# A Mamba-2 phase on one NeuronCore: the recurrence's products split, batched and moved a slot ahead

## What is computed

```python
x = x + 0.5 * ffn(layernorm(x)); x = x + mamba2(layernorm(x)); x = x + 0.5 * ffn(layernorm(x))

def mamba2(h):       # 64 heads of 64, state 128, 2 batches x 1024 tokens
    z, xBC, dt = split(h @ W_in.T)
    x, B, C = split(silu(conv4(xBC) + conv_b))
    # per chunk of tokens l, s <= l in the chunk, A_cum the running sum of dt * A:
    Y_diag = (C_l . B_s) * exp(A_cum_l - A_cum_s) @ (x * dt)
    states = B^T @ (exp(A_cum_end - A_cum) * x * dt)
    new    = prev * exp(A_cum_end) + states          # prev is zero before the first chunk
    Y_off  = exp(A_cum_l) * (C_l . prev)
    g = (Y_diag + Y_off + D * x) * silu(z)
    return rmsnorm(g) * norm_w @ W_out.T
```

## Time and profile before

| | |
|---|---|
| median of 3 runs | 2496.81 us (2495.47 to 2498.77) |
| the profiled execution, first to last instruction | 2493.7 us |
| Mamba phase within it | from 352.6 (first of its records) to about 2131 us |
| TensorE busy, whole span | 91% |
| VectorE, ScalarE, GpSimd busy | 69%, 58%, 59% |
| mean granted TensorE clock, share of full | 0.968 |

### The profile page before, as it was taken

The page is one execution under the profiler, slowest core; times in us unless marked ns, Lnnn a source line. Parts: engine busy times, 40 slices in busy tenths (PEclk is TensorE's granted clock), DMA queues, the critical chain, the costliest instruction groups (busy, mean ns, idle before and its releaser), DMA issues. The chain is left out here.

```text
span 2493.7 us, 44179 instructions
## 1 busy us (share of the span) xinstructions
PE 2278.8 (91%) x11910; PEld 1779.2 (71%) x11910; DVE 1725.5 (69%) x3562; ACT 1437.7 (58%) x2899; POOL 1474.0 (59%) x1306
## 2 busy tenths in 40 slices
PE   5799977999999999999888999999999998579997
PEld 3677765777777777777566777777777776358776
DVE  6432276788887878788877788878878787653226
ACT  5133326676676766776556776667767775413332
POOL 2876342666666666666426666666666665178533
PEclk8999989999999999999899999999999999689999
DMA  8665342332333334334213333343333332165545
GB/s 334 236 190 161 125 143 60 89 89 89 94 105 86 86 92 105 88 88 97 66 41 95 89 88 97 97 96 88 88 93 101 84 88 51 52 232 187 161 134 192
DMA packets 204905, 285.33 MB, mean 114 GB/s; under 512 B 16288, under 2 KB 148458, under 8 KB 204816
## 3 DMA queue, kind: packets, MB, share of 16 engines
q1 hardware_dynamic: 185936, 219.18, 31.6%
q0 software_dynamic: 18880, 65.02, 8.4%
HBM read 225.43 MB, written 58.72 MB: 114 GB/s over the span
## 5 line engine op out<-in xcount | busy, mean ns | idle before, releaser
L1306 POOL TENSOR_TENSOR mamba_mix<-mamba_mix,mamba_scores 128x512 f32<-128x512 f32 x256 | 330.8, 1292 | 272.8 <-ACT mamba_mix L1490 272.8
L1989 PE MATMUL mamba_p_proj<-mamba_xt_lo,mamba_in_hi 128*128 128x512 f32 x1056 | 462.2, 438 | 7.0 <-DVE mamba_xs L1683 5.2
L1990 PE MATMUL mamba_p_proj<-mamba_xt_hi,mamba_in_hi 128*128 128x512 f32 x1056 | 415.9, 394 | 0.0
L1991 PE MATMUL mamba_p_proj<-mamba_xt_hi,mamba_in_lo 128*128 128x512 f32 x1056 | 415.5, 394 | 0.0
L1486 ACT ACTIVATE mamba_mix<-mamba_cum_l,mamba_cum_g 128x128 f32<-128x128 f32 x1024 | 324.4, 389 | 0.6 <-issue 0.6
L1678 DVE SCALAR_TENSOR_TENSOR mamba_xs<-mamba_p_proj,mamba_taps,mamba_xs 128x511 f32<-128x511 f32 (+2 forms) x384 | 285.4, 743 | 36.3 <-ACT mamba_xs L1420 27.2
L1709 DVE TENSOR_TENSOR mamba_total<-mamba_p_out,mamba_total 128x512 f32<-128x512 f32 x256 | 177.0, 692 | 147.9 <-PE mamba_p_out L2025 143.3
L1300 POOL TENSOR_TENSOR mamba_xend<-mamba_xdt,mamba_to_end_g 128x512 f32<-128x512 f32 x128 | 160.8, 1257 | 198.8 <-DVE mamba_xdt L1736 198.8
L660 DVE TENSOR_TENSOR ffn_h<-ffn_p_gu,ffn_sil 128x256 f32<-128x256 f32 x110 | 46.9, 426 | 295.6 <-ACT ffn_sil L545 295.3
L1989 PEld LDWEIGHTS mamba_p_proj<-mamba_xt_lo,mamba_in_hi 128*128 128x128 f32 x1056 | 200.8, 190 | 62.2 <-issue 9.4
L1991 PEld LDWEIGHTS mamba_p_proj<-mamba_xt_hi,mamba_in_lo 128*128 128x128 f32 x1056 | 199.7, 189 | 45.0
(11 more groups left out here) (335 smaller groups left out, 5466.6 us busy)
## 6 DMA issues: line engine op xcount, KB each, us to landing
mamba_cum_l<-mamba_cum_rows SPq DMA_DIRECT2D x128, 512.0 KB, 5.9
mamba_rise<-mamba_exp_rows SPq DMA_DIRECT2D x256, 128.0 KB, 5.4
ffn_xs<-slots_in SPq DMA_DIRECT2D x78, 256.0 KB, 2.7
slots_out<-ffn_y SPq DMA_DIRECT2D x78, 256.0 KB, 2.4
mamba_raw_x<-in_t SPq DMA_DIRECT2D x34, 512.0 KB, 7.3
mamba_raw_z<-in_t SPq DMA_DIRECT2D x32, 512.0 KB, 8.0
mamba_raw_out<-out_t SPq DMA_DIRECT2D x32, 512.0 KB, 3.7
slots_out<-ffn_xs SPq DMA_DIRECT2D x1, 9984.0 KB, 41.9
```

The lines of the kernel that those rows point to most:

```text
L1306: pool.tensor_tensor(mix[:, c % 2, :, :], mix[:, c % 2, :, :], scores[:, b * CPB + c, :].unsqueeze(1).broadcast_to([P, GH, P]), ALU.mult). ...
L1989: pe.matmul(bank, in_hi[:, piece, kk, :], xt_lo[:, kk, c], start=(kk == 0), stop=False)
L1990: pe.matmul(bank, in_hi[:, piece, kk, :], xt_hi[:, kk, c], start=False, stop=False)
L1991: last = pe.matmul(bank, in_lo[:, piece, kk, :], xt_hi[:, kk, c], start=False, stop=(kk == KT - 1))
```

## The change

- `recur(c)` is split. `off(c)` issues the two products with the state, `start(c)` the 256-column one, and `diag(j)` the half-width products of chunks 2j and 2j + 1 together, eight in a row. `diag(0)` stands behind `project_x` tile 0, `diag(1)` behind `project_x` tile 1 (in slot 0 behind `project_z` tile 0).
- `off(0)` of b = 0 (state zero) and `start(3)` of b = 1 (state never read) go, with their `carry`, `decay_state`, `next_state` and the clearing of `state`; after a batch's first chunk of a group the state is a copy.
- `mix` gets four buffers, and ScalarE and GpSimd make the next unit's decays in this slot: `exponents(next, 0)`, `(1)`, `(2)`, `(3)` and `next_scores(0)` to `(3)`. Slot 0 makes six of them.
- The half-width products of a whole unit lie in `p_diag` (two banks), the state's in `p_off`, the upper half of `p_st`'s bank. `carry` covers the unit.
- VectorE: `carry_of(c)` and `next_state(c)` come first in the slot and again behind the three steps of `conv(0)`; the additions of D x are two of 512 columns (`add_skip`), behind `diag(1)`; `add_carry` is two of 512 columns (384 for b = 0). `stage` is split: `cum_g` is copied early in slot b = 1.
- ScalarE: `round_out` first, `high` of the two tiles on either side of `tap_x` tile 0. GpSimd: `this_out` early. SyncE: `load_cum` runs a slot ahead, so `load_in` now stands behind the load for the chunks 2 and 3 of the next b = 1.

The diff, cut (`decay_scores`, `exponents` and `decay_state` differ in indices and wait counts alone; `exponents` now waits for `s_diag` of the unit before):

```diff
@@ -1063,18 +1063,18 @@
-        mix = sb("mix", [P, 2, GH, P])
-        carry = sb("carry", [P, 2, CT, P])
+        mix = sb("mix", [P, CPB, GH, P])
+        carry = sb("carry", [P, CT, BLK])
...
+        p_diag = ps("p_diag", [P, CT, BLK])
+        p_off = p_st[:, GC:2 * GC].rearrange("p (h l) -> p h l", h=CT)
...
@@ -1342,38 +1351,45 @@
-                decay_state(0)
-                decay_scores(U, b, 1)
+                def next_scores(c):
...
+                if first:
+                    decay_scores(U, b, 2)
+                decay_x(k, gi, b, 1, first)
+                decay_state(k, gi, b, 1)
+                if first:
+                    decay_scores(U, b, 3)
                 clear(0)
                 next_z(0)
-                decay_x(k, gi, b, 1, first)
-                decay_state(1)
                 next_z(1)
-                decay_scores(U, b, 2)
+                this_out(0)
+                this_out(1)
                 clear(1)
-                this_out(0)
-                if last:
-                    this_out(1)
-                decay_state(2)
-                next_x(0)
-                decay_scores(U, b, 3)
+                decay_state(k, gi, b, 2)
+                next_scores(0)
+                if not first:
+                    add_squares(U - 1, 1 - b, 0, second)
+                next_scores(1)
+                if b == 0:
+                    decay_state(k, gi, b, 3)
                 clear(2)
                 if not first:
-                    add_squares(U - 1, 1 - b, 0, second)
+                    add_squares(U - 1, 1 - b, 1)
                 if last and k + 1 < batches:
                     first_dt(k + 1)
                     for ct in range(CT):
                         first_x(k + 1, 0, ct)
-                decay_state(3)
+                next_x(0)
+                next_scores(2)
                 clear(3)
-                if not first:
-                    add_squares(U - 1, 1 - b, 1)
-                if not last:
-                    this_out(1)
                 next_x(1)
+                if b == 0:
+                    decay_state(k, gi, 1, 0)
                 if not last:
                     decay_x(k, gn, bn, 0)
-                    decay_scores(U + 1, bn, 0)
+                next_scores(3)
...
@@ -1527,23 +1544,30 @@
+                if first:
+                    for c in (2, 3):
+                        exponents(k, gi, b, c, young=True)
+                if b == 1:
+                    for ct in range(CT):
+                        round_out(k, gi, U, ct, k == 0 and second)
                 if not first:
-                    for ct in range(CT):
-                        high(U - 1, gp, 1 - b, ct, second)
+                    high(U - 1, gp, 1 - b, 0, second)
                 if not last:
                     tap_x(k, gn, bn, 0, first)
-                exponents(k, gi, b, 2)
+                if not first:
+                    high(U - 1, gp, 1 - b, 1, second)
+                if not last:
+                    exponents(k, gn, bn, 0)
+                if b == 0 and not last_group:
+                    round_x(k, gi, V, 0)
+                if not last:
+                    exponents(k, gn, bn, 1)
+                    tap_x(k, gn, bn, 1, first)
                 if not first:
                     for ct in range(CT):
                         square(U - 1, 1 - b, ct)
-                if b == 1:
-                    for ct in range(CT):
-                        round_out(k, gi, U, ct, k == 0 and second)
-                elif not last_group:
-                    round_x(k, gi, V, 0)
                 if not last:
-                    tap_x(k, gn, bn, 1, first)
-                exponents(k, gi, b, 3)
+                    exponents(k, gn, bn, 2)
...
                     silu_z(U + 1, 1 - b, 1, first)
-                    exponents(k, gn, bn, 0)
-                    exponents(k, gn, bn, 1)
+                    exponents(k, gn, bn, 3)
...
@@ -1745,32 +1770,40 @@
-                def combine(c):
...
+                def carry_of(c):
+                    if (b, c) == (0, 0):
+                        return
+                    dve.wait_ge(s_st, U * CPB + c + 1)
+                    if c % 2 == 0 or (b, c) == (0, 1):
                         dve.wait_ge(s_rise[c // 2], U * 32 + 32)
...
+                    dve.tensor_tensor(carry[:, :, c * P:(c + 1) * P], p_off,
                                       rise[:, c // 2, :, c % 2 * P:(c % 2 + 1) * P], ALU.mult).then_inc(s_car, 1)
...
+                def next_state(c):
+                    if (b, c) == (NB - 1, CPB - 1):
+                        return
+                    ends = p_st[:, 0:GC].rearrange("p (h d) -> p h d", h=GH)
+                    dve.wait_ge(s_st, U * CPB + c + 1)
+                    if (b, c) == (0, 0):
+                        dve.tensor_copy(state[:, :, :], ends).then_inc(s_state, 1)
+                    else:
+                        dve.wait_ge(s_decayed, faded(k, gi, b, c))
+                        dve.tensor_tensor(state[:, :, :], ends, decayed[:, :, :], ALU.add).then_inc(s_state, 1)
+                def add_skip(ct):
+                    dve.wait_ge(s_diag, U * 2 + 2)
+                    dve.scalar_tensor_tensor(xs[:, b, ct, :], xs[:, b, ct, :], skip[:, bass.ds(gi * CT + ct, 1)],
+                                             p_diag[:, ct, :], ALU.mult, ALU.add).then_inc(s_y, 1)
+                def add_carry(ct):
+                    lo = (1 - b) * P
+                    dve.wait_ge(s_car, carried(k, gi, b, CPB - 1))
+                    dve.wait_ge(s_y, U * CT + ct + 1)
+                    dve.tensor_tensor(xs[:, b, ct, lo:BLK], xs[:, b, ct, lo:BLK], carry[:, ct, lo:BLK],
...
@@ -1798,40 +1831,43 @@
+                carry_of(0)
+                next_state(0)
                 if not first:
                     gate(k, gp, bp)
-                combine(0)
+                elif k > 0:
+                    finish(k - 1, range(6, T))
+                if b == 1 and not last:
+                    stage_cum(k, gn)
+                next_rows(0, 1)
+                next_stats(0)
+                conv(0, (1, 2, 3))
+                carry_of(1)
+                next_state(1)
                 if not first:
                     gate_low(U - 1, gp, 1 - b)
-                elif k > 0:
-                    finish(k - 1, range(6, T))
-                next_rows(0, 1)
-                conv(0, (1,))
-                next_stats(0)
-                add_carry(0)
-                combine(1)
-                conv(0, (2,))
-                conv(0, (3,))
-                add_carry(1)
                 next_rows(2, 3)
-                conv(1, (1,))
-                next_stats(1)
                 if last:
                     add_out(0)
-                combine(2)
+                add_skip(0)
+                carry_of(2)
+                next_state(2)
                 if last and not more:
                     add_out(1)
-                conv(1, (2, 3))
-                add_carry(2)
+                conv(1, (1, 2, 3))
+                next_stats(1)
                 next_rows(4, 5)
                 if more:
                     add_out(1)
-                combine(3)
+                add_skip(1)
+                carry_of(3)
+                next_state(3)
+                for ct in range(CT):
+                    add_carry(ct)
...
@@ -2059,28 +2096,44 @@
-                def recur(c):
...
+                def off(c):
+                    if (b, c) == (0, 0):
+                        return
                     s = (b * CPB + c) * P
...
+                    pe.wait_ge(s_state, carried(k, gi, b, c))
+                    if k > 0 or not (first and c == 1):
+                        pe.wait_ge(s_car, carried(k, gi, b, c) - 1)
                     for ct in range(CT):
...
+                        mm = pe.matmul(p_off[:, ct, :], state[:, 2 * ct:2 * ct + 2, :].rearrange("p h d -> p (h d)"),
+                                       bc[:, 1, s:s + P], start=True, stop=True)
+                    if (b, c) == (NB - 1, CPB - 1):
+                        mm.then_inc(s_st, 1)
+                def start(c):
+                    if (b, c) == (NB - 1, CPB - 1):
+                        return
+                    if (b, c) == (0, 0) and not first:
+                        pe.wait_ge(s_car, carried(k, gi, 0, 0))
                     if c % 2 == 0:
                         pe.wait_ge(s_xend, U * 2 + c // 2 + 1)
                     pe.matmul(p_st[:, 0:GC], b_rows[:, b * CPB + c, :],
                               xend[:, c, :, :].rearrange("p h d -> p (h d)"), start=True,
                               stop=True).then_inc(s_st, 1)
+                def diag(j):
+                    pe.wait_ge(s_mix, U * CPB + 2 * j + 2)
+                    pe.wait_ge(s_xdt, U * 2 + j + 1)
+                    if j == 0 and not first:
+                        pe.wait_ge(s_y, U * CT)
+                    for c in (2 * j, 2 * j + 1):
+                        for h in range(GH):
```

(23 more changed lines are left out.)

140 lines of the change are left out of this document (56 added, 84 removed).

## The result

| | before | after |
|---|---|---|
| median of four runs, us | 2497.1 (2495.5 to 2498.8) | 2405.1 (2402.2 to 2408.3) |
| profiled execution, us | 2493.7 | 2404.5 |
| slots 1 to 29, first and second batch, us | 738.5, 738.7 | 695.3, 697.8 |

What follows compares the result with a forecast made beforehand. TensorE, 91% busy, was taken as the bound: slots fall from 25.46 to 23.48 us, 115 us over 58 slots, plus 5, 1 and 4 at the ends, 125 in all, giving 2372 us; range 2343 to 2425.

Steps and rivals of the forecast that it cites:

- The forecast's floor: TensorE's loop slot without waits: 24.30 us before, less 0.43 and 0.74, gives 23.13.
- the removed terms: TensorE, one whole-width pair of eight and one L2081 of eight gone in two slots: 0.43 us a slot.
- the excursions: TensorE's changes to half width and back, four become two a slot: 2 x 0.37 = 0.74 us saved.
- what would show it: List of signs for right or wrong, such as slots 23.2 to 23.8 us apart and sixteen half-width records over 0.98 us.
- rival C: Eight half-width products over two banks no longer run in pairs: 1.74 us more a slot, 2473 us; chance 0.04.
- The waits for `mix` and the state: TensorE's waits for decayed scores and state: `mix` wait goes; no wait for the state at off(2) or off(3).
- Rival D: Slower: carry_of(1) and next_state(1), behind conv(0), come 5 us late; slot 27.2 us, total 2598; chance 0.05.
- VectorE's chain to `project_z` of tile 1: conv(1) ends 0.3 to 0.4 us late in slots b = 0, no wait in b = 1; 0.25 a slot booked, plus 0.1.
- the walk: Step-by-step timing of VectorE's instructions through a slot from TensorE's first start, ending with conv(1) at 14.1 us (b = 0).
- Rival A: VectorE's chain becomes the bound: gate_low 2.9 us, small steps 0.66, 1 us later in both slots; 2430 us; chance 0.17.
- The ends: Slots outside the loop: slot 30 gains 5 and 1 us, the last slots 4, slot 0 nothing (-3 to +3 each).
- the better case: No new wait and 2 us more from each batch's ends: 2345 us; chance 0.07.

Runs made afterwards that it cites:

- Carry late: Changed kernel with small steps of b = 1 last, add_skip(0) behind conv(1), conv(1)'s first step earlier, slots 0 and 30 reordered, add_carry(1) behind the second accumulation: 2355.0 us.
- edges: "Carry late" with repairs outside the loop, in slots 0 and 30 and at batch 1's finishing of batch 0's tiles: 2347.8 us, ratio 0.941 to before.
- gate first: "edges" with carry_of(0) and next_state(0) behind gate again: 2366.4 us, ratio 0.9404 to before, against 0.9408.
- GpSimd pauses: Changed kernel with one wait more: in slots b = 0 GpSimd stands behind its second product with the scores until conv(1) is done: 2419.4 us.
- skip late: Changed kernel with add_skip(0) moved from ahead of carry_of(2) to behind conv(1): 2404.4 us, ratio 0.963 to before.

## Why the prediction was right, and where it was off

**TensorE's own path: right.** The forecast's floor was 23.13 us. "Carry late" shows it without waits, in slots b = 1: 23.0. The parts hold one by one, the removed terms 0.43 against 0.46 and the excursions 0.74 against 0.70 a slot. Sixteen records took 1.02 us, where "what would show it" had 0.98 or so. The half-width products stayed in pairs, so rival C is out.

**The waits for `mix` and the state: right.** No wait for `mix` is left, and the state is late in slot 30 alone. Rival D, with its price of 4 us a slot, did not come: `next_state(1)` begins 7.46 us into the slot and ends at 7.9, as forecast. That the state moved ahead of `gate` has no part in it in the kernel "edges" ("gate first"); in the changed kernel itself this was not tried. That the decays are made a slot ahead was not undone by itself, so that this is what took the waits for `mix` away is argued, not shown.

**VectorE's chain to `project_z` of tile 1: this is the step that failed.** In slots b = 0 the walk had `conv(1)` begin at 11.2 us, and it began at 11.0. Then it gave `conv(1)` 2.9 us, with 0.3 for each small step. They took 0.29, 0.65 and 1.22, `conv(1)` 3.9. The earlier trace rows had shown a small step of 0.66, and the text set it aside as "the widest of them", as if the width were what it pays for, though it named GpSimd's part too. "GpSimd pauses" shows that it pays for GpSimd's instruction beside it. The term was 0.25 of waiting and 0.1 behind it, 0.35 a slot. By starts it was 1.40 in slots b = 0 of the first batch and about 0.45 in slots b = 1. Over all 58 slots, the second batch's 24.59 and the slots 1 among them, the mean is 24.02, so 1.0 above 23.0. That, against a floor lower by 0.13, is 1.02 - 0.35 - 0.13 = 0.54 a slot, and the loop gave 84 us instead of 115 (25.46 to 24.02 a slot, 1.45 instead of 1.98).

**Rival A was the one that half came.** It had the place and the cause, and the small steps at 0.66, but it needed `gate_low` at 2.9 (it was 1.76 and 2.18) and had both slots late by 1.0. Only slots b = 0 were, by the small steps alone. The forecast took the two conditions together, where one was enough. In slots b = 1 the chain ended at 13.9 us instead of the walk's 13.5, and 0.4 too late for `project_z`, because `carry_of(2)` waits for TensorE ("skip late"), which the walk had not seen: it made everything ahead of `conv(1)` one chain from the slot's start.

**The ends.** Forecast 10 us, found 6: slot 30 of the first batch 3.9 instead of 5, the last slots and what follows them 6.8 instead of 4, slot 0 -1.2 and -1.3, within the bounds given, and slot 30 of the second batch -2.4 instead of +1. In that slot all three small steps were held, 1.05, 1.22 and 0.64 us, TensorE waited 1.86 and ran eight products at the lower clock. With 84 from the loop that makes 90, and the spans differ by 89.2.

**VectorE's load** was to fall below 20.3 us a slot. It rose to 20.7: eight additions fewer, but those from SBUF to SBUF longer. The prediction took `add_carry` as the same number of columns; it is a quarter fewer in slots b = 0, and still took longer. A slip in its sums: the better case (no new wait, 2 us more from each batch's ends) adds up to 2348, not 2345, and nothing hangs on it.

## What to carry to other kernels

Cost a short instruction by what can hold it, not by its width: one whose inputs are both in SBUF can take as long as the GpSimd instruction beside it. Where an engine is late, list all its readers in order: here the same 1.4 us showed at a projection, at the transposes and at the output projection in turn, and only moving work that nobody was waiting for took it away. An order that is worth nothing in one version (the state ahead of `gate`) can be worth 15 us in the next, so a part's worth is the worth it has beside the others.

## What the runs showed of the hardware

- A VectorE step on 1 to 3 columns with both inputs in SBUF took 0.21 us with GpSimd idle and up to 1.22 us beside it, ending within 0.03 us of GpSimd's instruction. Steps of 509 to 511 columns with an input in PSUM took 0.73 to 0.75 either way. The Trainium skill says so of the two engines (SBUF — State Buffer, "Who interferes with whom"): an instruction of VectorE with at most one input in SBUF does not contend, outside the modes that use two ports, and one with two contends with a GpSimd instruction that reads SBUF. The trace agrees. The prediction had the rule in view for `add_carry` and did not put it to the small steps.
- GpSimd pays too: its product with the scores took 1.72 us where it began beside `gate_low` (two inputs in SBUF), and 1.28 beside the convolution's steps.
- A change from whole-width to half-width products and back cost TensorE 0.35 us, for four heads as for eight. Starts place most of it: 0.09 ahead of the first record, 0.04 behind the first pair, 0.10 ahead of the next whole-width product and 0.10 behind its first record. The Trainium skill says that a change of tiling mode drains TensorE (TensorEngine Tiling (Array Packing), "Key Properties"); it gives no figure.
- After waits of 2.93 and 1.86 us TensorE ran for some 3 us at the lower level of its clock, 0.43 us a product of 512 columns instead of 0.23; after waits of 1.47, once a slot, it did not. The length of the last wait does not tell it alone: slot 0 of the changed kernel has the same two waits, 1.51 and 1.68 us, in both batches, and the products behind them ran at granted clock 1.00 in the first (444 to 449 us) and 0.50 in the second (1281 to 1284 us). What came before differs: the second batch has a wait of 5.40 us at 1266.
